# Context projections of a decoder layer made ahead of the iterations that use them, and kept in DRAM

## The reference

```python
h = _ln(x)                                   # attention 1: one softmax over the positions per head
z = softmax(h @ W_A.T * 0.25, axis=1)        # 16 heads
out[i] = sum over j <= i of z[(i - j) % S] * (h @ W_V.T)[j]
x = x + out @ W_O.T + b_O
h = _ln(x)                                   # attention 2: over the context of the same sequence
score = (h @ WQ) @ (ctx @ WK).T / 16, causal mask
x = x + softmax(score) @ (ctx @ WV)
h = _ln(x)                                   # 2 shared and 16 routed experts, top 2 of a softmax
x = x + sum over experts of comb * (silu(h @ wg) * (h @ wu)) @ wd
```

## Time and profile before

| | us |
|---|---|
| median of 3 runs (672.47 to 674.39) | 674.21 |
| profiled execution, first to last instruction (span) | 672.6 |
| iterations 0 and 1 | 105.4 |
| each of iterations 3 to 7 | 73.3 |
| iteration 8 | 70.1 |
| iteration 9 | 55.7 |

### The profile page before, as it was taken

One profiled execution on the slowest core, in us unless ns is written; L12 is line 12 of the kernel. 1 busy time (PEld: TensorE's weight loads), 2 busy tenths in 40 slices (PEclk: granted clock), 3 DMA queues, 4 the chain that ended last, 5 costly groups with the idle time before them and its releaser, 6 DMA issues. The chain is left out here.

```text
span 672.6 us, 14191 instructions
## 1 busy us (share of the span) xinstructions
PE 582.0 (87%) x5212; PEld 389.0 (58%) x5212; DVE 486.3 (72%) x1133; ACT 222.8 (33%) x446; POOL 198.2 (29%) x221
## 2 busy tenths in 40 slices
PE   3338648998999899989999899989998989998796
PEld 2226426665775568556866567556855666665353
DVE  4656355868887788778787888788777867787574
ACT  3343113342334333442433333433334223322121
POOL 4312022225232342343322533234233320232132
PEclk9769576999999999999999999999999999999899
DMA  5887010391009500680029200860158002300500
GB/s 155 289 261 250 32 31 5 76 312 54 32 4 257 180 0 33 138 275 26 33 59 303 77 14 21 229 208 0 36 120 258 1 33 63 65 1 32 121 7 33
DMA packets 57201, 69.36 MB, mean 103 GB/s; under 512 B 2384, under 2 KB 46288, under 8 KB 56912
## 3 DMA queue, kind: packets, MB, share of 16 engines
q1 hardware_dynamic: 57168, 68.92, 35.8%
HBM read 64.13 MB, written 4.78 MB: 102 GB/s over the span
## 5 line engine op out<-in xcount | busy, mean ns | idle before, releaser
L464 POOL TENSOR_TENSOR mid<-gated,mid 128x512 f16<-128x512 f32 x80 | 95.0, 1188 | 196.6 <-ACT mid L589 196.6
L129 PE MATMUL wide<-w_d,mid 128*128 128x256 f16 x320 | 87.5, 273 | 4.7 <-POOL mid L464 4.1
L584 ACT ACTIVATE gated<-score 128x512 f32<-128x512 f32 x80 | 47.6, 595 | 129.1 <-PE score L131 115.2
L131 PE MATMUL wide<-w_d,mid 128*128 128x256 f16 x320 | 87.2, 273 | 0.0
L130 PE MATMUL wide<-w_d,mid 128*128 128x256 f16 x320 | 87.2, 273 | 0.0
L769 DVE TENSOR_TENSOR gated<-gated,stage 128x512 f32<-128x512 f32 x64 | 78.2, 1222 | 4.1 <-DMA stage<-comb_scratch 1.5
L763 DVE SCALAR_TENSOR_TENSOR gated<-gated,score 128x512 f32<-128x512 f32 x80 | 54.6, 682 | 33.4 <-ACT gated L584 32.2
L129 PE MATMUL rows<-h3T,w_gu 128*128 128x512 f16 x160 | 61.3, 383 | 12.9 <-DVE gated L772 11.7
L129 PE MATMUL score<-h3T,w_gu 128*128 128x512 f16 x160 | 60.9, 381 | 1.0 <-DVEq L109 1.0
L130 PE MATMUL rows<-h3T,w_gu 128*128 128x512 f16 x160 | 61.1, 382 | 0.0
L131 PE MATMUL rows<-h3T,w_gu 128*128 128x512 f16 x160 | 61.0, 381 | 0.0
(11 more groups left out here) (173 smaller groups left out, 1392.4 us busy)
## 6 DMA issues: line engine op xcount, KB each, us to landing
toep<-z_scratch SPq DMA_DIRECT2D x16, 2048.0 KB, 15.8
stage<-comb_scratch SPq DMA_DIRECT2D x32, 512.0 KB, 7.6
x_in<-in_x SPq DMA_DIRECT2D x8, 512.0 KB, 13.1
cT_in<-in_ctxT SPq DMA_DIRECT2D x8, 512.0 KB, 3.5
out<-x_out SPq DMA_DIRECT2D x8, 512.0 KB, 3.0
stage<-in_gu_r SPq DMA_DIRECT2D x1, 2048.0 KB, 11.1
stage<-in_wd_r SPq DMA_DIRECT2D x1, 1024.0 KB, 13.3
x_out<-in_gu_s SPq DMA_DIRECT2D x1, 512.0 KB, 6.3
```

The lines of the kernel that those rows point to most:

```text
L129: pe.matmul(out, stationary[0], moving[0], start=start, stop=False, **kw)
L131: return pe.matmul(out, stationary[1], moving[0], start=False, stop=stop, **kw)
L464: pool.tensor_tensor(mid[:, 1, j % SLOTS], gated[:, j % SLOTS], mid[:, 0, j % SLOTS], ALU.subtract).then_inc(mid_split.sem, 1)
L584: act.activation(gated[:, j % SLOTS], score.bank(f"g{j}")[:], ACT.Tanh, scale=0.5 / (X_H * X_W)).then_inc(tanh_done.sem, 1)
```

## The change

The projections of batch n's context are no longer made in iteration n + 1. Contexts 0 and 1 are projected in iteration 0, contexts 2 to 5 in iteration 1, 6 in iteration 2 and 7 in iteration 3. Each is four units of 12 or 6 matmuls into the halves of `wide`, split by ACT and DVE. Context 0 goes straight to `qT` and `vx`; the others go to buffers that are free at the time (`mixT`, `probT`, `stage`), from there to DRAM (`q_scratch`, `v_scratch`), and SP reads one batch back in each iteration (`fetch_context`). The loads of the weights stand ahead of that of x(1). The large weights are split in pieces. The expert stages run one further ahead of attention 2 (`AHEAD = 3`): stage 0 stands before o0, stages 1 and 2 before the turn of h2. Iterations 2 and 3 are written out, and the loop holds 4 to 6.

```diff
-SCORE = ["z", "g0", "g1", "s0", "s1", "g2", "s2", "g3", "s3", "g4", "g5", "g6", "g7", "g8", "g9", "none"]
-ROWS = (["logit", "v0", "v2", "x0", "o0", "o2", "x2", "u0", "u1", "u2", "u3", "p0", "u4", "p1", "u5", "p2"]
-        + ["u6", "p3", "u7", "u8", "u9", "none"])
+SCORE = ["z", "g0", "g1", "g2", "s0", "s1", "g3", "s2", "g4", "s3", "g5", "g6", "g7", "g8", "g9", "none"]
+ROWS = (["logit", "v0", "v2", "u0", "o0", "o2", "u1", "u2", "u3", "u4", "p0", "u5", "p1", "u6", "p2", "u7"]
+        + ["p3", "u8", "u9", "none"])
+AHEAD = 3
+CONTEXT_AT = {4: (3, (0, 1)), 5: (3, (2, 3)), 6: (4, (0, 1)), 7: (4, (2, 3)), 8: (5, (0, 1, 2, 3))}
+CONTEXT_IN = {2: 6, 3: 7}
...
+            def context(n, units):
+                if 0 in units:
+                    pe.wait_ge(c_split.sem, c_split.at(n, K2))
+                for u in units:
+                    if ctx_taken.at(n, u - 1) > 0:
+                        pe.wait_ge(ctx_taken.sem, ctx_taken.at(n, u - 1))
...
             def iteration(it, f, m, d, n, c=None):
+                first = f and m and not d
...
                 if m:
+                    pe.wait_ge(ctx_taken.sem, ctx_taken.at(1 if first else 5 if c == 6 else 6 if c == 7 else B - 1, UNITS))
                     toeplitz(it, it - 1, 0)
                     toeplitz(it, it - 1, 1)
...
-                if m:
-                    pe.wait_ge(c_split.sem, c_split.at(it - 1, K2))
-                    project(it, "x0", cT, w_vx)
+                if f and not m:
+                    context(0, range(UNITS))
+                if d and m:
+                    turn_comb(it)
+                if d:
+                    gate_up(it, 0)
+                if m:
                     pe.wait_ge(turned.taken.sem, turned.is_taken(it, "mix.1"))
                     project(it, "o0", mixT, w_o)
                     project(it, "o2", mixT, w_o)
-                    project(it, "x2", cT, w_vx)
...
+                if c is not None:
+                    context(c, range(UNITS))
+                if d:
+                    gate_up(it, 1)
+                if d and m:
+                    if c is not None:
+                        pe.wait_ge(ctx_taken.sem, ctx_taken.at(c, UNITS))
+                    down(it - 2, 0)
+                if d:
+                    gate_up(it, 2)
...
+                if first:
+                    context(2, range(UNITS))
                 if m:
                     pe.wait_ge(h_ready[1].sem, h_ready[1].at(it - 1, 1))
                     turn(it, "h2", h2)
-                if d:
-                    gate_up(it, 1)
-                if m:
-                    pe.wait_ge(q_split.sem, q_split.at(it - 1, 2))
+                if d and m:
+                    down(it - 2, 1)
+                if m:
+                    pe.wait_ge(ctx_loaded.sem, ctx_loaded.at(it - 1, 0))
...
                     scores(it, 0)
                     scores(it, 1)
...
+            def fetch_context(it, b):
+                if isinstance(b, int):
+                    sp.wait_ge(ctx_stored[b], 32)
+                sp.wait_ge(rows.ready.sem, rows.is_ready(it, "p3"))
+                sp.dma_start(qT[:].rearrange("p a k s -> p (a k s)"), q_dram[b]).then_inc(ctx_loaded.sem, 16)
+                sp.dma_start(vx[:].rearrange("p a c e -> p (a c e)"), v_dram[b]).then_inc(ctx_loaded.sem, 16)
```

436 lines of the change are left out of this document (281 added, 155 removed).

## The result

The changed kernel takes **662.5 us** (median of 4 runs, 660.5 to 663.9) against 674.0 of the kernel before in the same session (4 runs): a ratio of 0.983, 95% interval 0.981 to 0.985. It is 11.5 us faster. The forecast was 650.6 us, 23.6 us faster: the direction and the place of the gain are right, and about half of it is missing.

What follows compares the result with a forecast made beforehand. PE's stream was taken to bound steady iterations, waits to bound iterations 0 and 1. Terms -20.0 - 4.5 + 0.4 + 0 + 0.5 = -23.6 gave a span of 649.0, plus 1.6 to the median: 650.6 us, range 636 to 664.

Steps and rivals of the forecast that it cites:

- What bounds the kernel: Steady iteration, 73.3 us: PE's own stream sets the time; in iterations 0 and 1 the waits set it.
- Iterations 4 to 7: Steady iterations: 73.3 - 5.2 - 3.0 + 1.2 + 2.0 = 68.3 us, -5.0 each, -20.0 together.
- DVE's lag at a bank of `rows`: Steady iterations: PE's 1.9 us wait for DVE becomes 2.0, between 0.8 and 3.9 if the statistics are late in full.
- ACT's mid ahead of the tanh: Steady iterations: ACT's copy of `mid`, 0.62 us, now precedes the tanh, which comes about as late as before.
- Iteration 8: Iteration 8, with no next x and less of the old waits: -4.5 us.
- Iterations 2 and 3: Iterations 2 and 3 keep one projection through the halves of `wide`: +0.2 us each, +0.4 together.
- The start: Iterations 0 and 1, five more projections: loads and weights 0, h2 wait -2, contexts 3 to 5 +2; sum 0, -6 to +11.
- On the clock the argument: Start, from 69.9 us on, clock 0.60: moved matmuls would run at half speed, unless they themselves take the idling away.
- Iteration 9: Tail: the win at comb's turn is lost at the bank of stage 3's gate: +0.5 us, between -2.6 and +3.
- The start pays: Rival, iterations 0 and 1: the start costs its upper end, +11 us, total 662 us; chance 0.15.
- No new waits: Rival: DVE's 2.0 us lag goes with the `cT` copies, start gains 6; 15 us less, 636 us; chance 0.17.
- DVE becomes the bound: Rival, steady iterations: DVE's in-order waits keep 16 us, period 71, total 663 us; chance 0.12.

Runs made afterwards that it cites:

- the old order in the tail: Changed kernel with, in iteration 9 alone, comb's weighing before DVE's first gate and PE's turn of comb before expert stage 1: 657.0 us against 675.3.
- the kernel before with both edits: Kernel before with ACT's and POOL's context copies and differences in stages 8 and 9, and ACT's mid copy ahead of the tanh: 662.1 us against 672.9, ratio 0.984.
- the run with the tanh first: Changed kernel with ACT's tanh of a stage ahead of its copy of mid again, from stage 3 on: 676.5 us against 675.3 of the kernel before.

## Why the prediction was half right, step by step

The forecast was -23.6 us and -11.5 were measured. Three terms failed: the waits of the steady iterations (a wait before the turn of comb put at nothing), the tail (a bank's wait of 5.3 us priced as 0.5), and the start (the waits before the turn of mix and o0, and the price of the moved projections as a whole). None of the signs of being wrong that were named appeared: the period is not over 70, iteration 2 starts between 100 and 112 us, and nothing waits for the reloads.

- **What bounds the kernel.** Right in the steady state: the two waits that were removed there in the changed kernel, before the turn of comb and before the scores, shortened iteration 6 by their size. One sentence went too far: that a matmul taken out of PE's stream is worth what it takes. In the kernel before it was worth less than nothing (the run without most projections). The -5.2 us of PE came true in a kernel that put other stages into the gap. The prediction took that order as given and did not see that it could be the condition.
- **Iterations 4 to 7: the step that failed, -16.4 for -20.0.** Period 69.3 for 68.3, by these terms: PE's work -5.15 (forecast -5.2); the wait before the scores 1.4 (1.2, right); DVE's lag at a bank of `rows` 0.9 (2.0, and not from the statistics, which the run with them moved showed). Not in the sum at all: 0.9 before the turn of comb, where PE catches DVE between weighing and the low part of mixT, and 0.6 and 0.5 at the turns, of which I had let the old 0.6 go. These three are 2.0 us against 1.1 that the bank's wait was better. That the turn of comb had moved ahead of stage 0 stood in the diff; I costed it at nothing without asking how far DVE would be. The 0.5 stands before the turn of h2, and the trace shows something there that the prediction did not look at: DVE's normalisation takes 1.0 us longer than in the kernel before, and POOL's bias additions run beside all four of its steps, where they ran beside two. Changed kernel first, DVE and POOL, then the kernel before:

```profile
417.01 2.86 DVE L808 TENSOR_SCALAR h<-x_res,mean_var,rstd 128x256 f32<-128x256 f32 x4 [0.30 <-POOL rstd L531]
416.79 2.93 POOL L543 TENSOR_TENSOR x_bo<-x_in,b_o 128x256 f32<-128x256 f32 x4
```
```profile
421.44 1.82 DVE L695 TENSOR_SCALAR h<-x_res,mean_var,rstd 128x256 f32<-128x256 f32 x4
```

  No run moves these additions away, so what they cost the iteration is not shown.
- **ACT's mid ahead of the tanh.** Wrong in sign. With it, fewer of DVE's multiplications run beside POOL's difference, and its undoing costs 1.9 us an iteration.
- **Iteration 8**, -2.4 for -4.5 in the profiled execution. The clock decides here. Five other kernels have the same iteration 8: in three it took 65.8 to 66.1 us (-4.0 to -4.3), in two 67.7, as in this one. Here are the 10 us from the turn of comb on, this execution first, then that with the old order in the tail, which took 66.1:

```profile
543.30:553.30 10.00, 9.43 (x50) 0.83 0.50 112
```
```profile
542.50:552.50 10.00, 9.44 (x63) 1.00 0.49 124
```

  The waits ahead of it are the same in both. So the term was right but for 1.7 us of clock, which some executions pay and others don't (the kernel before with both edits paid them in its iteration 8, too).
- **Iterations 2 and 3**, +0.2 for +0.4: right. No wait for the reloads appeared, either.
- **The start**, 0: +2.6 in this execution; over nine kernels iteration 2 started at 107.1 to 110.3. Toeplitz matmuls at 45.3 for 45.5 and the three contexts at 2.7 for 2 were right. From the first Toeplitz matmul to iteration 2 it took 62.7 us for 59.3. The wait ahead of h2 fell from 3.8 to 1.2 us (forecast -2), and contexts 3 to 5 cost their 2.7. What failed is the step up to o0: PE waits 1.5 us before the turn of mix and 1.4 for 0.2 before o0, 2.7 us more, for which the forecast had 0.6 (the lead of the Toeplitz matmuls given back). Not ACT's copies cause it, as it was put there: with them behind mix nothing was gained. 0.6 us more are left open. In all, the kernel before has iteration 2 at 105.4 and with its loads reordered had it at 99.7, so against that execution five projections, 26 us of PE, with their copies cost 7 to 11 us. By the medians' 3.2 us for the loads it is 5 to 8. Both the gain of the loads and the price of the projections were larger than forecast, and that they nearly cancelled is luck. On the clock the argument held. From 70 to 81 us it was 0.50, and from 81 to 108 us, where contexts 3 to 5 stand, 0.96, before 0.60 over the whole, and 0.63 in the run without most of them. The Trainium skill's rule on bursts between idling ("TensorE: Matmul & The Clock Gate", section "HAM oscillation — how this bites in real kernels") is borne out where the waits stayed, in the piece at 0.50 and behind the 5.29 us in the tail, and did not apply where the moved work filled them.
- **Iteration 9**, +0.5 for +5.4 (2.7 to 6.1 by execution): the other step that failed. The mechanism was named (the bank of stage 3's gate stands behind the wait for the comb rows), and its price was wrong. The comb rows come 1.2 us later, 20.4 for 19.2 us after the start, since a gate stands ahead of the weighing. The bank was expected to give back what the turn won (1.8 us), and its wait is 5.3 us, where the kernel before has 1.0 (before stage 2's gate): more than twice that. And behind so long a wait PE runs at about half clock, for more or less of the next 10 us. The bank alone is not the cause, either: with it counted early the wait moved to the next gate, and only the old order took most of it away.
- **The rivals.** None became the case. "The start pays" had the right total, 662 us, by the wrong way: the start took 2.6 of its 11 us. "No new waits" was right that much of DVE's lag came from the copies of `cT` (1.0 of 1.9, by the run that moved them). "DVE becomes the bound" was not seen in the changed kernel's steady iterations; something like it shows in the kernel before with both edits, where the second one's gain went from one wait into another.

The sum of the terms was off by 13.1 us: 4.9 in the tail, 5.7 in iterations 4 to 8, 2.6 in the start, less 0.2 in iterations 2 and 3. The three have one sign. They are waits that I had not seen, and what is not seen enters a sum as nothing; on top, in iteration 8 and in the tail, comes the clock, which differs between executions.

## What to carry to other kernels

Before taking work out of the busiest engine's stream, ask which chain it covers: leave the work out in a trial and read the waits, which here showed a loss of 10 us where 8 x 4.8 = 38 us of matmuls were left out. Then try edits of order alone. Two of them, the context's two copies and two differences moved to the last stages and ACT's copy of mid put ahead of the tanh, gave the kernel before as much as the whole change, with its seven contexts put through DRAM, gave; and the change has both of these edits in it. With its further waits removed the changed kernel reached 646.3 us. How far the kernel before would come by the same treatment was not tried. After an edit, list the engine's waits again and remove them one at a time; a wait before which two instructions of the releasing engine could be swapped costs one line.

## What the runs showed of the hardware

- **DVE's multiplication of two f32 tiles beside POOL's subtraction.** Alone it takes 0.69 us, beside POOL up to 1.54. From the run with the tanh first, start and duration:

```profile
449.61 1.16 POOL L536 TENSOR_TENSOR mid<-gated,mid 128x512 f16<-128x512 f32 x1 [5.11 <-ACT mid L681]
449.77 1.54 DVE L883 TENSOR_TENSOR gated<-gated,stage 128x512 f32<-128x512 f32 x1
```

  POOL's ends at 450.77, DVE's at 451.31, so DVE got little done before POOL was through: 1.54 is about the 1.00 us until POOL's end and most of its own 0.69. The Trainium skill ("SBUF — State Buffer", section "Who interferes with whom") has a DVE instruction with two SBUF inputs and a GpSimd instruction that reads SBUF shut each other out for a whole instruction; the trace agrees, to 0.15 us. The same work costs DVE 9.1 us in one order of ACT and 6.3 in the other (eight multiplications), 5.5 in the kernel before with both edits.
- **DVE's normalisation beside POOL.** The four steps over 128x256 f32 take 1.38 us alone, 2.86 beside four bias additions of POOL and 3.07 beside two of its subtractions (rows above). An order that frees the multiplications can load the normalisations, which stand closer to what PE waits for.
- **The clock falls behind a single wait of 4.0 us** in an iteration that is otherwise dense (0.83 over 10 us, in the kernel before without most projections). Behind the wait for g3 in the tail it was 0.52 (5.29 us of wait) in one execution and 0.81 (4.95 us) in that of a kernel with the same tail; the stretch from the comb rows to the end took 40.7 and 38.4 us.
- **It can fall without a long wait.** In iteration 8 of the changed kernel the clock is 0.50 from 543.8 to 547.2 us. In the 10 us before, no wait is over 1.0 us, and PE was busy for 7.2 us. Of six executions with this iteration 8 three show the fall, at the price of 1.7 us, and three don't, with the same waits before it. In the steady iterations, with waits of up to 1.9 us, it is 1.00 throughout.
